# Two one-hot comparisons on VectorE: one wide operation of two tensors, or one operation a tile against a column of scalars

## The chip, the cores and the metric

The kernel runs on one core of one Trainium2 chip. The metric is the device time of one execution in microseconds; of the kernel before there are three, and their median is 2625.97 us. The profile is one more execution, recorded by the hardware.

## The reference, cut to what matters

A layer norm of x (12500 nodes, 256 features), a graph part and a feed-forward part with four experts, each with a residual:

```
time_feat = relu(edge_attr @ W_time.T + b_time)          # 212500 edges, 64 features
sums   = segment_sum(time_feat, src, num_segments=n)     # by the edge's source node
counts = segment_sum(ones, src, num_segments=n)
node_time_feat = sums / maximum(counts, 1)
fused = relu(concat(node_feat, node_time_feat) @ W_fusion.T + b_fusion)
x = x + (ln(x) + fused @ W_up.T + b_up)
x = x + shared_mlp(ln(x)) + top-2 of 4 experts(ln(x))
```

The change lies in the segment sum alone. `src` of this call is a list in no order that could be used as a segment order directly, so the kernel groups edges by bucket of 256 nodes.

## The kernel before

Edges are padded to 1664 tiles of 128. Two tiles make a group (256 edges), four groups a step, so there are 208 steps (`NS`) of eight tiles. Within a group VectorE sorts the edges by bucket (`sort_step`, lines 953 and 954 are its exchanges), which gives each edge a slot; three slots make one row of the table in DRAM.

All engines run one loop of 208 steps and meet through semaphores. In step s:

- VectorE prepares step s + 1 in `one_hots`: first `begun` (line 1119), for each of 4 groups a 128x128 matrix that says whether a bucket's blocks have begun at a row; then `slot_hot` (line 1127), for each of 8 tiles a 128x384 one-hot matrix of the edge's slot. Both compare a row of counted numbers in float16 (`iota_16`) with one number a partition and tile: the slot codes in `codes`, the beginnings in `begin`. The codes are written by ScalarE (line 1384) from PSUM, the beginnings by VectorE (line 860). Three buffers of each (`NSLOT`) let VectorE run ahead; `slot_hot` waits for TensorE's moves of three steps ago.
- TensorE computes features (line 597), takes high parts off (line 615), moves edges into their slots with `slot_hot` as the weights (line 611, six matmuls a group), and finds the rows of the table with `begun` (line 624).
- ScalarE applies the relu in three parts (line 1372), copies the moved rows out of PSUM (`keep_rows`, line 1378) into one of 12 buffers and the rows' numbers (`keep_dest`, line 1392) into one of 4.
- GpSimd issues four indirect DMAs a step (line 1564) that scatter the moved rows into the table. It also issues 36 that zero the ends of the tables (line 1553). Before a row buffer is written again, its scatter must have landed.
- From step 56 on, SyncE loads finished parts of the table, VectorE makes one-hots of the node within the bucket (line 1031), TensorE sums with them (line 640), and VectorE adds the sums (line 1051), in turns that `turn_at` spreads over the steps.

In the first steps VectorE also counts buckets (`count_bucket`, line 929), an operation of one tensor of 2-byte numbers and a constant, in runs of four without a wait between them. After the loop come the rest of the turns, and then from about 1757 us the node part in 25 groups, where line 1300 normalizes with two column scalars and line 1313 masks bits.

The order on every engine is that of the code; only waits move it in time. The two comparisons before are written as operations of two tensors, where the second repeats a pair of equal float16 numbers (`pairs`, `each_pair`, `in_pairs`): that is why `codes` and `begin` hold every number twice.

Of the kernel before, what the change touches and what calls it, by code (L numbers as in the profile page):

```python
# [6 lines left out]
P = 128  # L7
# [4 lines left out]
BLOCK = 3  # L12
# [13 lines left out]
def gnn_ffn(nc, x, src_e, src_g, attr, weights, dims, out):  # L26
    f32r, f16, u16 = mybir.dt.float32r, mybir.dt.float16, mybir.dt.uint16
    f32, bf16, i32 = mybir.dt.float32, mybir.dt.bfloat16, mybir.dt.int32
    ALU, ACT, AX = mybir.AluOpType, mybir.ActivationFunctionType, mybir.AxisListType
# [6 lines left out]
    GT, GS, GP = TILES_A_GROUP, GROUPS_A_STEP, GROUPS_A_SET  # L36
    G = GT * P
    NGR = ET // GT
    TS = GT * GS
# [13 lines left out]
    parts = [(set_cuts[k] * SPS, set_cuts[k + 1] * SPS) for k in range(NPARTS)]  # L53
    part_of = [k for k, (s0, s1) in enumerate(parts) for _ in range(s0, s1)]
    ng = [(s1 - s0) * GS for s0, s1 in parts]
# [30 lines left out]
    with ExitStack() as ctx:  # L86
# [7 lines left out]
        NATTR, NPAY, NROWS, NDEST, NTB, NSLOT, NXA, NIB = 3, 3, 12, 4, 4, 3, 3, 4  # L94
# [16 lines left out]
        s_slot, s_begun, s_dest_ps, s_dest, s_moved, s_rows = (sem(f"s_{n}") for n in ("slot", "begun", "dest_ps", "dest", "moved", "rows"))  # L111
# [75 lines left out]
        def carve(shape, dt, partitions=P):  # L187
            free = int(np.prod(shape))
            words = free if dt in (f32, i32) else (free + 1) // 2
            a = arena[0:partitions, top[0]:top[0] + words]  # L190
            top[0] += words
            assert top[0] <= ARENA, top[0]
            if dt != f32:
                a = a.bitcast(dt)[:, 0:free]
            if len(shape) == 1:
                return a
            names = "abcd"[:len(shape)]
            return a.rearrange(f"p ({' '.join(names)}) -> p {' '.join(names)}",
                               **dict(zip(names[1:], shape[1:])))

        hi = carve([ET], bf16)
        lo = carve([ET], bf16)
        codes = carve([NGR, GT, 2], f16)
        keys = carve([G, SETS], u16, GP)
        idx_key = carve([G], f32, GP)
        NGM, NCM = max(ng), max(n_ch)
# [2 lines left out]
        blocks_to = carve([NGM], f32)  # L209
        zeros_row = carve([NGM], f32)  # L210
        place = cnt_i.bitcast(f32)
        begin = [carve([n, 2], f16) for n in ng]
        hop = [carve([n, 2], bf16) for n in ng]
        col_i = carve([2], i32)
        col_f = carve([6], f32)
# [21 lines left out]
        iota_16 = carve([BLOCK * P], f16)  # L237
        slot_hot = [carve([TS, BLOCK * P], f16) for _ in range(NSLOT)]
        begun = [carve([GS, P], f16) for _ in range(NSLOT)]
# [80 lines left out]
        bank = [moved[:, 512 * i:512 * (i + 1)] for i in range(4)] + [ctx.enter_context(nc.psum_tensor(f"bank{i}", [P, 512], f32)) for i in range(4, 8)]  # L320

        def b3d(a, n, m):

            return a.unsqueeze(2).to_broadcast([a.shape[0], n, m])
# [5 lines left out]
        def pairs(a, n):  # L330
            return a.rearrange("p (c u) -> p c u", u=2).unsqueeze(1).to_broadcast([P, n, a.shape[1] // 2, 2])

        def each_pair(a, n):
            return a.unsqueeze(2).to_broadcast([P, a.shape[1], n // 2, 2])

        def in_pairs(a):
            return a.rearrange("p t (c u) -> p t c u", u=2)
# [88 lines left out]
        ZB, SB, MB = 4, (5, 6), 7  # L426
# [393 lines left out]
        def vector_program(e):  # L820
            def size_step(k, i):
                ps, n, m = bank[SB[0]], ng[k], n_ch[k]

                def sized(ins):
                    return ins.then_inc(s_size, 1)
# [31 lines left out]
                elif i == 9:  # L857
                    after("first")
                    sized(e.tensor_scalar(col_f[:, 3:4], col_f[:, 2:3], float(CH), None, ALU.mult))
                    sized(e.tensor_copy(begin[k], b3d(ps[:, 0:n], n, 2)))  # L860
                elif i == 10:
                    after("row0")
                    sized(e.scalar_tensor_tensor(place[:, 0:n], blocks_to[:, 0:n], col_f[:, 3:4], n_blocks[:, 0:n], ALU.add, ALU.subtract))
# [223 lines left out]
            for q in attr_in:  # L1087
                ins = e.memset(q[ONES_AT:ONES_AT + 1], 1.0)
# [23 lines left out]
            def one_hots(s):  # L1112
                k = part_of[s]
                if s == parts[k][0]:
                    e.wait_ge(s_size, size_no(k, "begin"))
                if s >= NSLOT:
                    e.wait_ge(s_dest_ps, s - NSLOT + 1)
                begin4 = begin[k][:, GS * (s - parts[k][0]):GS * (s - parts[k][0] + 1), :]
                e.tensor_tensor(in_pairs(begun[s % NSLOT]), pairs(iota_16[:, 0:P], GS), each_pair(begin4, P), ALU.is_ge).then_inc(s_begun, 1)
                if s % SPS == 0:  # L1120
                    e.wait_ge(s_codes, s // SPS + 1)
                if s == 0:
                    e.wait_ge(s_const, 2)
                if s >= NSLOT:
                    e.wait_ge(s_moved, GS * (s - NSLOT + 1))
                code8 = codes.rearrange("p g j u -> p (g j) u")[:, s * TS:(s + 1) * TS, :]
                e.tensor_tensor(in_pairs(slot_hot[s % NSLOT]), pairs(iota_16, TS), each_pair(code8, BLOCK * P), ALU.is_equal).then_inc(s_slot, 1)  # L1127

            one_hots(0)
            for step in range(n_steps):  # L1130
# [239 lines left out]
        def scalar_program(e):  # L1370
# [9 lines left out]
            def keep_codes(b, q):  # L1380
                q += sort_cuts[b]
                e.wait_ge(s_code_ps, q + 1)
                for j in range(GT):
                    ins = e.activation(codes[:, q * GP:(q + 1) * GP, j, :], b3d(bank[MB][:, j * GP:(j + 1) * GP], GP, 2), ACT.Copy)
                ins.then_inc(s_codes, 1)

            def keep_dest(s):
# [292 lines left out]
```

## Time and profile before

| | |
|---|---|
| median of 3 runs | 2625.97 us (2618.89 to 2632.24) |
| profiled execution, span of its instructions | 2387.8 us |
| outside of the span (median less span) | 238.2 us |
| TensorE matmul busy | 2163.3 us (91%) |
| VectorE busy | 1819.8 us (76%), 5481 instructions |
| ScalarE busy | 1324.4 us (55%) |
| GpSimd busy | 1222.2 us (51%), 944 instructions |

The profiled execution has no total of its own beside its span; what lies around the span is taken as the median less the span. In the tables of the trace, PE is TensorE, DVE VectorE, ACT ScalarE, POOL GpSimd and SP SyncE. A share of busy time is a mean over stages: GpSimd's 51% is made of some 1420 us in which it issues scatters and some 900 us in which it does almost nothing. Durations of VectorE instructions overlap a little: the next one's start is recorded before the end of the one ahead, so what an instruction costs its engine is the distance of two starts.

### The profile page before, as it was taken

How to read it: one execution, taken by the hardware profiler on the slowest of the kernel's cores; microseconds unless marked ns; L12 is line 12 of the kernel's file. 1: busy time of each engine (PE TensorE's matmuls, PEld its weight loads, DVE VectorE, ACT ScalarE, POOL GpSimd, SP SyncE). 2: the span in 40 equal slices, each digit the busy share in tenths (PEclk: the TensorE clock that was granted, in tenths of full speed). 3: DMA queues.
4: the chain of work that ended last, by engine and by line, in shares of the span. 5: the costliest groups of instructions: out<-in, count | busy, mean ns of one | idle time of the engine just before them, and what ended most of it. 6: DMA issues, size and time to landing. Idle time of an engine off the chain costs nothing.

```text
span 2387.8 us, 76843 instructions
## 1 busy us (share of the span) xinstructions
PE 2163.3 (91%) x28773; PEld 1798.7 (75%) x28773; DVE 1819.8 (76%) x5481; ACT 1324.4 (55%) x2833; POOL 1222.2 (51%) x944
## 2 busy tenths in 40 slices
PE   5778887789999999899999998888879999999998
PEld 1666665588988888799999998778756666676676
DVE  9987664687888987699998886899956656666565
ACT  1667776677878777777777776000023434344343
POOL 0787887888887888777788777000011111111110
PEclk7888988899999999999999999999989999999999
DMA  2263535456766666677777775777721111111111
GB/s 77 87 165 123 155 116 144 151 166 188 213 200 202 182 189 182 191 223 219 207 224 220 220 218 164 209 206 208 207 66 47 54 40 57 44 40 60 41 40 36
DMA packets 244429, 345.06 MB, mean 145 GB/s; under 512 B 34526, under 2 KB 218516, under 8 KB 243352
## 3 DMA queue, kind: packets, MB, share of 16 engines
q1 hardware_dynamic: 201252, 228.82, 35.0%
q0 software_dynamic: 42576, 110.49, 13.9%
q8 instruction: 232, 3.80, 0.7%
q14 instruction: 135, 1.11, 0.2%
q10 hardware_dynamic: 234, 0.85, 0.1%
HBM read 200.75 MB, written 186.38 MB: 162 GB/s over the span
## 4 chain that ended last, share of the span: by engine, by line
PE 60%; DMA 12%; issue 8%; DVE 8%; POOL 5%; ACT 4%; DVEq 2%; SPq 0%; POOLq 0%; ACTq 0%
PE bank L640 13%; PE moved L611 11%; PE bank L727 9%; DMA table<-arena 7%; PE moved L740 6%; PE bank L597 5%; POOL table L1564 4%; DMA arena<-table 4%; PE bank L615 3%; PE bank L735 2%; ACT arena L1378 2%; PE bank L813 2%; PE bank L769 2%; DVEq L1034 2%; ACT arena L1372 1%
## 5 line engine op out<-in xcount | busy, mean ns | idle before, releaser
L1564 POOL DMA_INDIRECT table<-arena x832 | 1093.8, 1315 | 338.7 <-issue 275.9
L1378 ACT ACTIVATE arena<-moved 128x588 bf16<-128x588 f32 x832 | 546.0, 662 | 193.3 <-PE moved L611 117.5
L611 PE MATMUL moved<-arena 128*128 128x196 bf16 x4992 | 602.5, 258 | 11.9 <-ACT arena L1378 10.8
L611 PEld LDWEIGHTS moved<-arena 128*128 128x128 f16 x4992 | 460.8, 99 | 94.8 <-ACT arena L1378 29.0
L1372 ACT ACTIVATE arena<-bank 128x512 f32<-128x512 f32 x624 | 372.2, 596 | 153.6 <-PE bank L597 124.9
L1127 DVE TENSOR_TENSOR arena<-arena 128x3072 f16<-128x3072 f16 x208 | 364.6, 1753 | 113.7 <-PE moved L611 112.4
L1051 DVE TENSOR_TENSOR sums<-sums,bank 128x130 f32 x912 | 259.0, 284 | 133.2 <-PE bank L640 120.3
L640 PE MATMUL bank<-arena 128*128 128x65 bf16 x8208 | 312.8, 194 | 34.7 <-DVE arena L1031 16.5
L640 PE MATMUL bank<-arena,w_all 128*128 128x65 bf16 x8208 | 309.9, 193 | 19.5 <-DVE sums L1051 10.1
L640 PEld LDWEIGHTS bank<-arena 128*128 128x128 bf16 x8208 | 290.7, 98 | 41.7 <-DVE arena L1031 30.3
L640 PEld LDWEIGHTS bank<-arena,w_all 128*128 128x128 bf16 x8208 | 288.3, 98 | 25.8 <-issue 12.9
L1031 DVE TENSOR_TENSOR arena<-arena 128x768 bf16<-128x768 bf16 x456 | 251.3, 552 | 33.6 <-DMA arena<-table 32.9
L1580 POOL TENSOR_TENSOR arena<-arena 128x4 f32<-128x4 f32 (+1 forms) x25 | 25.2, 1006 | 485.1 <-DVE arena L1287 485.1
L1031 DVE TENSOR_TENSOR w_all<-arena 128x768 bf16<-128x768 bf16 x456 | 250.9, 551 | 6.2 <-DMA arena<-table 5.9
L1468 ACT ACTIVATE arena<-bank,w_all 128x512 f32<-128x512 f32 (+1 forms) x225 | 152.9, 680 | 183.1 <-PE bank L727 145.1
L615 PE MATMUL bank<-arena,minus_ident 128*128 128x512 bf16 x416 | 172.4, 414 | 89.4 <-ACT arena L1372 88.7
L597 PE MATMUL bank<-w_all,arena 97*128 97x192 f32 (+1 forms) x1248 | 243.3, 333 | 3.5 <-ACT arena L1372 2.5
L1571 POOL TENSOR_TENSOR arena<-arena,w_all 128x1024 f32<-128x1024 f32 (+1 forms) x25 | 57.5, 2301 | 301.8 <-DMA arena<-x_ln 259.6
L597 PEld LDWEIGHTS bank<-w_all,arena 97*128 97x128 f32 x1248 | 208.1, 198 | 5.1 <-issue 3.4
L1482 ACT ACTIVATE arena<-bank 64x512 f32<-64x512 f32 (+1 forms) x25 | 14.2, 570 | 262.3 <-PE bank L754 262.3
L740 PE MATMUL moved<-w_all,arena 128*128 128x256 f32 x588 | 151.8, 403 | 1.2 <-DVE arena L1305 1.2
L727 PE MATMUL bank<-yt_high,w_high 128*128 128x512 f32 (+1 forms) x300 | 135.5, 452 | 0.0
(223 smaller groups left out, 2867.2 us busy)
## 6 DMA issues: line engine op xcount, KB each, us to landing
arena<-table SPq DMA_DIRECT2D x304, 441.0 KB
arena<-in_attr SPq DMA_DIRECT2D x208, 144.0 KB
table<-arena POOLq DMA_INDIRECT x832
x_ln<-arena SPq DMA_DIRECT2D x98, 128.0 KB
arena<-in_x SPq DMA_DIRECT2D x97, 128.0 KB
arena<-x_ln SPq DMA_DIRECT2D x24, 512.0 KB, 4.6
out_rows<-arena SPq DMA_DIRECT2D x24, 512.0 KB, 3.3
fused_node<-arena SPq DMA_DIRECT2D x98, 32.0 KB
```

Source lines behind the costliest of these rows:

```text
L597: mm = e.matmul(bank[ZB][:, q * 3 * A:q * 3 * A + w], attr_in[s % NATTR][0:ONES_AT + 1, q, :], wt[:, 0:w], start=q == 0, stop=True, skip_g ...
L611: mm = e.matmul(moved8[:, 4 * (n % 2) + h, 0:PW], slot_hot[s % NSLOT][:, t, h * P:(h + 1) * P], upper(s, 0, PW)[:, t, :], start=j == 0, st ...
L615: return e.matmul(z, minus_ident[:], upper(s, c0, A), start=False, stop=True, skip_group_check=True)
L640: mm = e.matmul(ps[:, v * SW:v * SW + w], one_hot, tab[t % NTB][:, c, r, c0 + at:c0 + at + w], start=i == 0 and at == 0, stop=i == CR * BL ...
L727: mm = e.matmul(bank[BH[(u - 1) % 2]][:, 0:w], weight(a, k), yt_halves[b][:, k, 0:w], start=i == 0, stop=i == len(terms) - 1)
L740: mm = e.matmul(half(BO, t), lhs[:, t * P:(t + 1) * P], rhs, start=first and t % 2 == 0, stop=done, skip_group_check=True)
L1031: e.tensor_tensor(in_pairs(hot[t % 2][:, c * PIECE:(c + 1) * PIECE]), pairs(iota_lo, PIECE), each_pair(lo_of, NODES_A_BUCKET), ALU.is_equa ...
L1051: e.tensor_tensor(d, d, sum_bank(t, c), ALU.add).then_inc(s_added, 1)
L1127: e.tensor_tensor(in_pairs(slot_hot[s % NSLOT]), pairs(iota_16, TS), each_pair(code8, BLOCK * P), ALU.is_equal).then_inc(s_slot, 1)
L1372: return e.activation(part_of_pay(s, c0, A), z, ACT.Relu)
L1378: e.activation(row_buf[n % NROWS], moved8[:, 4 * (n % 2):4 * (n % 2) + 3, 0:PW], ACT.Copy).then_inc(s_rows, 1)
L1564: e.indirect_dma_start(out=tables[k], out_offset=bass.IndirectOffsetOnAxis(ap=dest[s % NDEST][:, a:a + 1], axis=0), in_=row_buf[n % NROWS] ...
```

## The change

The two comparisons become operations of one tensor (`iota_16`) and one fp32 scalar a partition, read from a column of memory: 4 of 128 columns in place of one of 512 for `begun`, 8 of 384 in place of one of 3072 for `slot_hot`. Each run of them signals once, after its last. `codes` and `begin` hold each number once, in fp32, in as much memory as before; so ScalarE's copy of the codes and VectorE's copy of the beginnings write half the numbers.

```diff
-        codes = carve([NGR, GT, 2], f16)
+        codes = carve([NGR, GT], f32)
...
-        begin = [carve([n, 2], f16) for n in ng]
+        begin = [carve([n], f32) for n in ng]
...
-                    sized(e.tensor_copy(begin[k], b3d(ps[:, 0:n], n, 2)))
+                    sized(e.tensor_copy(begin[k], ps[:, 0:n]))
...
-                begin4 = begin[k][:, GS * (s - parts[k][0]):GS * (s - parts[k][0] + 1), :]
-                e.tensor_tensor(in_pairs(begun[s % NSLOT]), pairs(iota_16[:, 0:P], GS), each_pair(begin4, P), ALU.is_ge).then_inc(s_begun, 1)
+                for a in range(GS):
+                    g = GS * (s - parts[k][0]) + a
+                    ins = e.tensor_scalar(begun[s % NSLOT][:, a, :], iota_16[:, 0:P], begin[k][:, g:g + 1], None, ALU.is_ge)
+                ins.then_inc(s_begun, 1)
...
-                code8 = codes.rearrange("p g j u -> p (g j) u")[:, s * TS:(s + 1) * TS, :]
-                e.tensor_tensor(in_pairs(slot_hot[s % NSLOT]), pairs(iota_16, TS), each_pair(code8, BLOCK * P), ALU.is_equal).then_inc(s_slot, 1)
+                code8 = codes.rearrange("p g j -> p (g j)")[:, s * TS:(s + 1) * TS]
+                for t in range(TS):
+                    ins = e.tensor_scalar(slot_hot[s % NSLOT][:, t, :], iota_16, code8[:, t:t + 1], None, ALU.is_equal)
+                ins.then_inc(s_slot, 1)
...
-                    ins = e.activation(codes[:, q * GP:(q + 1) * GP, j, :], b3d(bank[MB][:, j * GP:(j + 1) * GP], GP, 2), ACT.Copy)
+                    ins = e.activation(codes[:, q * GP:(q + 1) * GP, j], bank[MB][:, j * GP:(j + 1) * GP], ACT.Copy)
```

On VectorE, at the loop's beginning (the first three steps' one-hots; the two lines between belong to the keys of the later sorts):

```order
-L1119 TENSOR_TENSOR arena<-arena 128x512
-L1127 TENSOR_TENSOR arena<-arena 128x3072
-L1119 TENSOR_TENSOR arena<-arena 128x512
-L1127 TENSOR_TENSOR arena<-arena 128x3072
-L1139 TENSOR_SCALAR arena<-arena 104x1792
-L1141 TENSOR_TENSOR arena<-arena 104x7x256
+L1120 TENSOR_SCALAR arena<-arena 128x128 x4
+L1130 TENSOR_SCALAR arena<-arena 128x384 x8
+L1120 TENSOR_SCALAR arena<-arena 128x128 x4
+L1130 TENSOR_SCALAR arena<-arena 128x384 x8
+L1143 TENSOR_SCALAR arena<-arena 104x1792
+L1145 TENSOR_TENSOR arena<-arena 104x7x256
```

Nothing changes its place; each pair of instructions becomes a run of 12 (an "x4" or "x8" is as many instructions in a row). On VectorE in a step with turns, first before and then now (line 1051 adds the sums of one chunk, line 1031 makes a one-hot, line 1049 keeps a register):

```order
L1051 TENSOR_TENSOR sums<-sums,bank 128x130
L1031 TENSOR_TENSOR w_all<-arena 128x768
L1034 TENSOR_LOAD offs
L1119 TENSOR_TENSOR arena<-arena 128x512
L1127 TENSOR_TENSOR arena<-arena 128x3072
L1049 ISA
L1051 TENSOR_TENSOR sums<-sums,bank 128x130
```

```order
L1051 TENSOR_TENSOR sums<-sums,bank 128x130
L1031 TENSOR_TENSOR w_all<-arena 128x768
L1034 TENSOR_LOAD offs
L1120 TENSOR_SCALAR arena<-arena 128x128 x4
L1130 TENSOR_SCALAR arena<-arena 128x384 x8
L1049 ISA
L1051 TENSOR_TENSOR sums<-sums,bank 128x130
```

Here too the run stands where the pair stood, and no other engine's order changes.

## Rows read from the trace of the kernel before

**Rows 1.** The page's 40 equal slices (59.7 us each): busy tenths of two engines.

```profile
PE   5778887789999999899999998888879999999998
...
POOL 0787887888887888777788777000011111111110
```

**Rows 2.** Stretches: from:to and length in us, busy us (instructions) by engine, then clock.

```profile
core 0: us, PE busy (x) PEld busy (x) DVE busy (x) ACT busy (x) POOL busy (x), PEclk, DMA share, GB/s
60.00:300.00 240.00, 190.18 (x1595) 150.55 (x1593) 192.52 (x492) 163.75 (x366) 192.27 (x142) 0.89 0.48 132
300.00:600.00 300.00, 246.33 (x2923) 208.39 (x2924) 199.84 (x487) 216.87 (x486) 243.92 (x185) 0.90 0.52 154
600.00:900.00 300.00, 284.95 (x4772) 261.70 (x4770) 264.82 (x666) 235.55 (x532) 244.53 (x183) 0.99 0.68 198
900.00:1200.00 300.00, 287.90 (x5001) 265.71 (x4998) 258.79 (x681) 231.40 (x520) 234.29 (x185) 0.99 0.70 205
1200.00:1475.00 275.00, 274.95 (x5117) 259.22 (x5115) 232.63 (x566) 206.03 (x458) 211.81 (x167) 1.00 0.75 216
```

**Rows 3.** The scatters on the page: count, busy us, mean ns, idle before them; then min/median/max.

```profile
L1564 POOL DMA_INDIRECT table<-arena x832 | 1093.8, 1315 | 338.7 <-issue 275.9
...
L1564 POOL DMA_INDIRECT table<-arena x832: 967/1034/7097, 64.8 to 1489.0; - x167
```

**Rows 4.** Waits (us, times, longest): POOL's in 300:900, then ACT's in 60:900.

```profile
POOL table L1564 <- issue: 87.2, 286, 0.3
...
ACT arena L1378 <- DMA table<-arena: 72.2, 54, 5.8
```

**Rows 5.** VectorE's groups by shape: busy us, mean ns, idle before and its releaser.

```profile
L1127 DVE TENSOR_TENSOR arena<-arena 128x3072 f16<-128x3072 f16 x208 | 364.6, 1753 | 113.7 <-PE moved L611 112.4 <-ACT arena L1384 1.3
...
L1119 DVE TENSOR_TENSOR arena<-arena 128x512 f16<-128x512 f16 x208 | 87.2, 419 | 0.7 <-issue 0.6
...
L1300 DVE TENSOR_SCALAR arena<-arena 128x256 f32<-128x256 f32 x98 | 33.8, 407 | 1.2 <-POOL arena L1580 1.2
...
L929 DVE TENSOR_SCALAR arena<-arena 128x624 bf16<-128x624 bf16 x98 | 24.9, 317 | 0.0
...
L929 DVE TENSOR_SCALAR arena<-arena 128x416 bf16<-128x416 bf16 x49 | 12.8, 261 | 0.0
...
L1313 DVE TENSOR_SCALAR arena<-arena 128x256 int32<-128x256 int32 x2 | 0.6, 286 | 0.0
```

**Rows 6.** VectorE in order of time near 83 us: start, duration, instruction, count.

```profile
82.34 1.01 DVE L929 TENSOR_SCALAR arena<-arena 128x624 bf16<-128x624 bf16 x4
83.27 0.42 DVE L1119 TENSOR_TENSOR arena<-arena 128x512 f16<-128x512 f16 x1
83.60 1.75 DVE L1127 TENSOR_TENSOR arena<-arena 128x3072 f16<-128x3072 f16 x1
```

**Rows 7.** VectorE and POOL in order of time near 1015 us.

```profile
1014.37 1.75 DVE L1127 TENSOR_TENSOR arena<-arena 128x3072 f16<-128x3072 f16 x1
...
1014.60 2.37 POOL L1564 DMA_INDIRECT table<-arena  x1 [0.30 <-issue]
```

**Rows 8.** The same beside a run of line 929, near 103 us.

```profile
102.77 1.01 DVE L929 TENSOR_SCALAR arena<-arena 128x624 bf16<-128x624 bf16 x4
...
102.42 1.49 POOL L1564 DMA_INDIRECT table<-arena  x1 [0.30 <-issue]
```

**Rows 9.** The same near 127 us.

```profile
126.06 1.01 DVE L929 TENSOR_SCALAR arena<-arena 128x624 bf16<-128x624 bf16 x4
126.98 0.42 DVE L1119 TENSOR_TENSOR arena<-arena 128x512 f16<-128x512 f16 x1
127.32 1.75 DVE L1127 TENSOR_TENSOR arena<-arena 128x3072 f16<-128x3072 f16 x1
...
126.17 3.74 POOL L1564 DMA_INDIRECT table<-arena  x1 [0.30 <-issue]
```

**Rows 10.** The same near 242 us.

```profile
241.26 0.98 DVE L929 TENSOR_SCALAR arena<-arena 128x624 bf16<-128x624 bf16 x4
...
241.62 1.01 POOL L1564 DMA_INDIRECT table<-arena  x1 [0.30 <-issue]
```

## The prediction

> **What bounds the kernel now.** I read the page's slices first. TensorE and GpSimd are both busy from about 60 to 1475 us; after that GpSimd is almost idle [rows 1]. The changed operations run only in these 1415 us, so what the change is worth is decided there. The table by stretches says more [rows 2]. GpSimd is busy 680.7 us of the 840 between 60 and 900 us, in 510 instructions. That looks like room, but each of its DMA instructions is preceded by 0.30 us in which it waits for nothing (the bracket in [rows 7]). Its waits of 300 to 900 us have 0.3 as the longest, so it never waits for data there [rows 4]. 510 x 0.30 = 153 us, and 680.7 + 153 = 834 of 840 us: GpSimd is full from 60 to 900 us. ScalarE meanwhile waits 72.2 us for scatters to land before it may reuse a row buffer [rows 4], and TensorE waits for ScalarE. From 900 to 1475 us GpSimd takes 446.1 + 352 x 0.30 = 551.7 of 575 us: 23 us are free, and TensorE, busy 563 of these 575 us, is the bound.
>
> In steps: four scatters a step. 60 to 900 us has 510 DMAs, about 37 of them for the tables' ends, so 473 / 4 = 118 steps; 900 to 1475 us has 352 / 4 = 88.
>
> Then VectorE. Its idle time is 540 - 392 = 148 us in 60 to 600 us and 875 - 756 = 119 us in 600 to 1475 us [rows 2], about 1.9 and 0.9 us a step. It runs ahead of TensorE: line 1127 waits 112.4 us in total for the moves that free its buffer [rows 5].
>
> **VectorE's own cost.** Line 929, one tensor of 2-byte numbers and a constant, takes 317 ns for 624 columns and 261 ns for 416 [rows 5]: 0.269 ns a column and 149 ns fixed. Four in a row start 0.93 us before what follows [rows 6], 0.233 each, so 84 ns of each duration lie under the next. The scalar from memory is priced by line 1300, 256 columns of fp32 with two such scalars, 407 ns, against line 1313, 256 columns of 4 bytes with none, 286 ns: 60 ns a scalar. So
> - 384 columns: 149 + 103 + 60 - 84 = 228 ns, x8 = 1.83 us, for 1.753 - 0.084 = 1.67 us before;
> - 128 columns: 149 + 34 + 60 - 84 = 159 ns, x4 = 0.64 us, for 0.33 us before [rows 6].
>
> Together 2.47 for 2.00 us, +0.47 us a step, 98 us in 208 steps. No row has a float16 tensor with an fp32 column. From below, a free scalar makes it 1.34 + 0.40 = 1.74 us (-0.26 a step). From above, half line 929's rate (2 columns where it has 4, as line 1313 has with 4-byte numbers) makes it 8 x 332 + 4 x 194 = 3.43 us (+1.43). I take 2.47: line 929 has the same sizes of elements, and line 1300 shows that a scalar adds a fixed term and leaves the rate of its 4-byte numbers alone.
>
> 0.47 is under VectorE's mean idle time of 0.9 or 1.9 us a step, and its buffers carry it over steps in which the sort fills it. What is exposed: about 1 us at the start, where TensorE waits for the first one-hots, and 2 or 3 us where sorting and turns meet. If that cover were gone (0.47 against 0.9), it costs up to 98 us.
>
> Line 860 (three times) and ScalarE's line 1384 (16 times) write half as many numbers: cast at nothing, bounds 0 and -2 us. The DMAs and waits stay where they are. The waits inside `one_hots` stand ahead of the first instruction of each run, so nothing new is queued behind them; the signal comes with the run's last instruction, which is in the sum above.
>
> **What the run does to GpSimd.** This is the term that decides. A scatter lasts 967 ns at least and 1315 on average [rows 3]. The excess, 348 ns x 832 = 290 us, has a visible cause. The scatter that starts 0.23 us after line 1127 lasts 2.37 us and ends at 1016.97, 0.85 us after line 1127 has ended [rows 7]. So a scatter touches something at its start that line 1127 holds, and does its 0.85 us of work when that is given back. Line 1127 comes 208 times and scatters follow each other every 1.27 us, so the first start falls on average 0.64 us into its 1.75 us: some 1.1 us of waiting a step. The excess of four scatters is 1.39 us a step in all, and other lines have a part in it; I take 1.0 us a step for the old pair.
>
> How does a run of one-tensor operations hold GpSimd? Line 929 is the only such run beside scatters.
> - It holds a scatter's end too: the one at 102.42 would have finished at 103.39, but ended at 103.91, 0.13 us after the run of four [rows 8]. Line 1127 doesn't do that.
> - It isn't given back between instructions of the run: at 103.27 a scatter should have reached its last part, an instruction of the run ended at about 103.55 and the wait went on. The scatter at 126.17 started inside a run and ended at 129.91, 0.84 us after line 1127 that followed it [rows 9].
> - It isn't strict: the scatter at 241.62 started inside a run and took 1.01 us [rows 10].
>
> The new run is 2.5 us long. With a touch at the start and one 0.85 us later, every 1.27 us, the first touch falls on average (0.85² + 0.42²) / (2 x 1.27) = 0.35 us into the run, and if nothing is given back it waits 2.5 + 0.1 - 0.35 = 2.2 us. I take 1.8, since some get through as in [rows 10]; that is an estimate. The bounds are 0.3 us (given back at each end, below) and 2.2 us. Against 1.0 us before, GpSimd takes +0.8 us more a step (-0.7 to +1.2).
>
> The sum: 118 steps in which GpSimd is full, x 0.8 = +94 us; 88 steps x 0.8 = 70, less the free 23, = +47 us; VectorE's start and dense places +3 us. +144 us on a span of 2387.8 is 2532; with the 238 us around the span, taken as unchanged, 2770 us. The longer steps also cover VectorE's 0.47.
>
> The Trainium skill (SBUF — State Buffer, SBUF: two separate sides) has VectorE and GpSimd share one pair of ports under an exclusive lock, taken by whichever starts first and held for the whole instruction. By it an instruction of 0.3 us is a wait of 0.3 at most. That the lock exists and that two tensors hold only GpSimd's reads agrees with [rows 7, 8]; that it ends with the instruction doesn't agree with [rows 9]. It is the first rival.
>
> **The rivals.**
> 1. The port is given back at the end of each instruction (faster). An operation of 0.31 us then holds a scatter 0.15 us on average, twice a step, 0.3 for 1.0 us before: GpSimd gains 0.7 us a step. Of 76 steps up to 600 us, 53 us come back, where TensorE is busy only 437 of 540 us. From 600 us TensorE is busy 94% and more, and 10 us are left to gain, which VectorE's 0.47 about eats. 2626 - 53 - 10 + 12 = 2575 us. For it: [rows 10], and the fixed 130 of 228 ns in which such an instruction hardly moves data. Against it: [rows 8, 9].
> 2. The scalar column halves the rate (slower still). The run is 3.4 us, it holds about 2.6 us, +1.6 a step: 208 x 1.6 - 23 = +310 us, 2935 us. Against it: line 1300 keeps the rate of its kind.
> 3. Nothing to be seen. The run is given back now and then, so that it holds about the 1.0 us of before, and VectorE's 0.47 lies in idle time: 2626 + 3 = 2629 us. For it: the mixed rows of line 929.
>
> The change does what it says, since the instructions can be seen in the order; that it would not isn't a case here.
>
> **The chances.** Forecast (held through most of the run) 0.58, its own range 2680 to 2870; rival 1 0.22; rival 2 0.07; rival 3 0.13. The predicted time is 2770 us. The range for 8 in 10 goes from 2570, about the middle of rival 1, to 2870: the forecast with the full 2.2 us, 208 x 1.2 - 23 = +227, gives 2853. No change is anything within 0.5% (13 us), about what a measurement of this kernel can tell. Slower: 0.58 + 0.07 + 0.03 of rival 3 = 0.68. Same: 0.10. Faster: 0.22.
>
> **What would show it.** Instructions of about 312 and 243 ns in lines 1130 and 1120, starts 228 and 159 ns apart; 560 ns or 400 ns mean rival 2's rate. The mean of a scatter at about 1315 + 200 = 1515 ns, and scatters that end 0.1 or 0.85 us after the run's last instruction; a mean near 1140 ns and no long ones is rival 1, one near 1315 rival 3. The slices should show GpSimd busy later than 1475 us, to some 1620, with TensorE's tenths lower in the same steps, and the node part after the loop as long as before (some 630 us). VectorE's waits for moves should be about as long as before or longer, since its cover grows. The forecast is wrong if the scatters' mean falls, or if the time moves while it stays.

## The result, and the profile after

The changed kernel takes 2701.8 us (median of 4 runs, 2695.45 to 2710.16), the kernel before 2626.5 on the same chip: 1.0305 times, 95% interval 1.0271 to 1.034. It is slower, as forecast, and by half of what was forecast (2770 us, 1.055 times).

The kernel before itself took 2382 to 2393 us in three comparisons, each on a chip of its own, and 2626 and 2665 us in two others, and the change does not do the same in both kinds; below they are called chips without and with stalls, though whether it is the chip is not shown.

The page after, first the slices (67.7 us each) that answer to [rows 1], then its chain and its groups. In the groups the columns are those of [rows 3] and [rows 5]:

```profile
PE   5678777788888888788888888878887999999999
...
POOL 0665555555554555454555554530000111111110
...
PE 61%; issue 9%; ACT 8%; DVE 7%; another core or an unknown queue 7%; DMA 4%; DVEq 1%; POOL 1%; SPq 0%; ACTq 0%; POOLq 0%
...
L1568 POOL DMA_INDIRECT table<-arena x832 | 908.7, 1092 | 850.0 <-ACT arena L1382 584.0
...
L1376 ACT ACTIVATE arena<-bank 128x512 f32<-128x512 f32 x624 | 373.3, 598 | 372.0 <-remote 223.1
```

GpSimd was to become fuller. It is emptier: its tenths fall from 7 or 8 to 5, a scatter takes 1092 ns on average for 1315 [rows 3], and its waits for ScalarE, none of which was over 0.3 us from 300 to 900 us, are 190.4 us there and 584 us in the whole run. Its last scatter ends at 1810 us, not at 1490. By its own sign the forecast is wrong here: the mean of the scatters falls. ScalarE in its turn waits for something that the trace calls remote, a source that it can't name; in the trace of before there was none of it. The same window as the POOL row of [rows 4] (waits from 300 to 900 us: sum, times, longest), and TensorE's from 60 to 2000 us:

```profile
POOL table L1568 <- ACT arena L1382: 190.4, 100, 5.6
POOL table L1568 <- issue: 72.0, 196, 1.4
...
PE bank L640 <- issue: 104.8, 234, 1.2
...
PE bank L597 <- issue: 13.4, 34, 1.1
```

TensorE is idle 104.8 us ahead of plain matmuls of line 640, 234 times, while it waits for nothing that the profile shows. Stretches that answer to [rows 2]:

```profile
300.00:600.00 300.00, 223.78 (x2096) 179.08 (x2097) 183.42 (x757) 189.29 (x418) 170.41 (x166) 0.84 0.42 126
600.00:900.00 300.00, 254.58 (x3818) 219.27 (x3817) 226.16 (x888) 190.69 (x429) 161.96 (x149) 0.97 0.52 160
900.00:1200.00 300.00, 250.38 (x3557) 213.27 (x3555) 224.19 (x844) 187.80 (x426) 157.84 (x146) 0.95 0.48 148
```

All four engines do less per 300 us than before [rows 2], so none of them is the bound that took over. VectorE's own rows, by shape and in order of time, answer to [rows 5, 6, 7]:

```profile
L1130 DVE TENSOR_SCALAR arena<-arena 128x384 f16<-128x384 f16 x1664 | 424.7, 327 | 155.8 <-PE moved L611 115.6 <-remote 33.2 <-issue 5.8
L1120 DVE TENSOR_SCALAR arena<-arena 128x128 f16<-128x128 f16 x832 | 171.1, 280 | 0.3 <-issue 0.2
```

```profile
1000.21 0.95 DVE L1120 TENSOR_SCALAR arena<-arena 128x128 f16<-128x128 f16 x4
1000.86 2.15 DVE L1130 TENSOR_SCALAR arena<-arena 128x384 f16<-128x384 f16 x8
1001.44 0.97 POOL L1568 DMA_INDIRECT table<-arena  x1 [0.30 <-issue]
...
1002.93 0.41 DVE L953 TENSOR_TENSOR arena<-arena 104x256 f32<-104x256 f32 x1
```

Four begun comparisons take 1000.86 - 1000.21 = 0.65 us (0.64 forecast), eight slot comparisons 1002.93 - 1000.86 = 2.07 us (1.83 forecast; 0.26 each, not 0.228). The scatter at 1001.44 starts in the middle of that run and takes its least time, 0.97 us. The forecast had it held to the end. That scatter is also why the run is long: in this trace 16 runs of eight have no scatter beside them, and they last 1.93 us at the median, so 1.85 us without the 0.08 us under the next instruction, as forecast.

### The profile page after: what moved, and what is told of

It is laid out like the page before. It is cut to its first block, busy times and chain, and to the rows that moved or that the text cites. A ratio compares the mean times of both kernels' runs of the same rounds, so it can differ in the third digit from the quotient of the medians.

```text
span 2708.4 us, 78923 instructions
## 1 busy us (share of the span) xinstructions
PE 2306.0 (85%) x28773; PEld 1863.2 (69%) x28773; DVE 1950.4 (72%) x7561; ACT 1325.9 (49%) x2833; POOL 1030.9 (38%) x944
## 4 chain that ended last, share of the span: by engine, by line
PE 61%; issue 9%; ACT 8%; DVE 7%; another core or an unknown queue 7%; DMA 4%; DVEq 1%; POOL 1%; SPq 0%; ACTq 0%; POOLq 0%
PE moved L611 13%; PE bank L640 12%; PE bank L727 8%; PE moved L740 6%; PE bank L597 6%; PE bank L615 3%; DMA arena<-table 3%; ACT arena L1382 3%; PE bank L624 2%; ACT arena L1376 2%; PE bank L735 2%; PE bank L813 2%; PE bank L769 2%; DVEq L1034 1%
## 5 line engine op out<-in xcount | busy, mean ns | idle before, releaser
L1568 POOL DMA_INDIRECT table<-arena x832 | 908.7, 1092 | 850.0 <-ACT arena L1382 584.0
L611 PE MATMUL moved<-arena 128*128 128x196 bf16 x4992 | 629.6, 264 | 40.5 <-ACT arena L1382 28.9
L1130 DVE TENSOR_SCALAR arena<-arena 128x384 f16<-128x384 f16 x1664 | 424.7, 327 | 155.8 <-PE moved L611 115.6
L640 PE MATMUL bank<-arena 128*128 128x65 bf16 x8208 | 339.4, 195 | 79.0 <-issue 55.0
L640 PE MATMUL bank<-arena,w_all 128*128 128x65 bf16 x8208 | 333.6, 194 | 66.8 <-issue 52.9
L640 PEld LDWEIGHTS bank<-arena 128*128 128x128 bf16 x8208 | 304.3, 99 | 98.3 <-issue 74.9
L597 PE MATMUL bank<-w_all,arena 97*128 97x192 f32 (+1 forms) x1248 | 274.4, 357 | 21.5 <-issue 13.4
L597 PEld LDWEIGHTS bank<-w_all,arena 97*128 97x128 f32 x1248 | 229.3, 215 | 35.1 <-issue 32.9
L1120 DVE TENSOR_SCALAR arena<-arena 128x128 f16<-128x128 f16 x832 | 171.1, 280 | 0.3 <-issue 0.2
L615 PEld LDWEIGHTS bank<-arena,minus_ident 128*128 128x128 bf16 x416 | 41.3, 99 | 148.9 <-ACT arena L1376 108.7
```

Source lines behind the costliest of these rows:

```text
L597: mm = e.matmul(bank[ZB][:, q * 3 * A:q * 3 * A + w], attr_in[s % NATTR][0:ONES_AT + 1, q, :], wt[:, 0:w], start=q == 0, stop=True, skip_g ...
L611: mm = e.matmul(moved8[:, 4 * (n % 2) + h, 0:PW], slot_hot[s % NSLOT][:, t, h * P:(h + 1) * P], upper(s, 0, PW)[:, t, :], start=j == 0, st ...
L615: return e.matmul(z, minus_ident[:], upper(s, c0, A), start=False, stop=True, skip_group_check=True)
L640: mm = e.matmul(ps[:, v * SW:v * SW + w], one_hot, tab[t % NTB][:, c, r, c0 + at:c0 + at + w], start=i == 0 and at == 0, stop=i == CR * BL ...
L1130: ins = e.tensor_scalar(slot_hot[s % NSLOT][:, t, :], iota_16, code8[:, t:t + 1], None, ALU.is_equal)
L1568: e.indirect_dma_start(out=tables[k], out_offset=bass.IndirectOffsetOnAxis(ap=dest[s % NDEST][:, a:a + 1], axis=0), in_=row_buf[n % NROWS] ...
```

## The experiments

Each ratio is to the kernel before on the same chip, with its 95% interval; "traced span" is that of the one profiled execution.

**The kernel before, again.** No edit.

> The kernel before, unchanged, for a second profile of it on a chip it shares with the next three. Open after the first comparison: the profiled execution of before had a span of 2387.8 us beside a median of 2626.5 us, the one of after a span of 2708.4 us beside a time of 2710.2 us. Theory A (the 238 us lie outside the span): the new span is near 2390 us again and its time near 2626. Theory B (the first profile of before was of an unusually quick execution): the new span is near 2620 us, and it shows the stalls that after has, in which TensorE waits for nothing that the profile shows (0.4 to 1.2 us before line 640) and ScalarE waits for an unknown releaser. I expect B, at 0.8. Ratio 1.00.

Measured: 2388.18 us, traced span 2389.1; the 19 runs of before on this chip have a median of 2391.57. Neither expectation fits. There is nothing outside the span here, and in the changed kernel's traced run the time is 2710.16 for a span of 2708.4. So the 238 us that the prediction put around the span do not exist: the trace shown was of an execution near 2390 us, the times shown were of others.

**The slot comparison alone.** `begin` and line 1119 stay as before:

```
-                e.tensor_tensor(in_pairs(slot_hot[s % NSLOT]), pairs(iota_16, TS), each_pair(code8, BLOCK * P), ALU.is_equal).then_inc(s_slot, 1)
+                for t in range(TS):
+                    ins = e.tensor_scalar(slot_hot[s % NSLOT][:, t, :], iota_16, code8[:, t:t + 1], None, ALU.is_equal)
+                ins.then_inc(s_slot, 1)
```

> Only the slot comparison as 8 operations of one tensor and a column; the beginnings stay one operation of two tensors. VectorE pays 8 x 0.23 for 1.67 us. Theory port (GpSimd held through runs): most of the 3.05%, since the longest run stays: +2 to 2.5%. Theory instruction count (more instructions on VectorE delay the fetching of all engines' instructions): 7 of 11 added instructions a step, +1.9%. Theory VectorE time (its own 0.47 us a step decide): 0.17 of 0.47 us, +1.1%.

Measured: 2314.78 us, 0.9675 (0.9657 to 0.9693). All three theories had it slower, and all three are wrong on this chip. Scatters 1105 ns on average; before on this chip 1332.

**The begun comparison alone.** The edit of the diff at lines 1118 to 1121, with `codes` as before.

> Only the comparison of beginnings as 4 operations of one tensor and a column; slots stay as before. Theory port: a run of 0.65 us ahead of the old 1.75, up to +1%. Theory instruction count: 3 of 10 or 11 added instructions a step, +0.8 to 0.9%. Theory VectorE time: 0.3 of 0.47 us, +2%.

Measured: 2383.88 us, 0.997 (0.9954 to 0.9985), scatters 1312 ns. Only the port theory's "up to +1%" comes near: by itself this part is almost nothing.

**Two tensors, by the tile.** The same twelve instructions a step as the change, but each still of two tensors:

```
+                for t in range(TS):
+                    ins = e.tensor_tensor(in_pairs(slot_hot[s % NSLOT][:, t:t + 1]), pairs(iota_16, 1), each_pair(code8[:, t:t + 1], BLOCK * P), ALU.is_equal)
```

> The kernel before with its two operations of two tensors cut by group and tile: 4 + 8 instructions of two tensors, as many instructions as after, about 2.65 us of VectorE a step (8 x 0.265 + 4 x 0.13) for 2.47 in after, and no one-tensor run. Theory port by one-tensor runs: near 1.00 or below, since short pieces free GpSimd more often. Theory instruction count, or VectorE time: 1.03 to 1.035, as after. This run tells the one-tensor form apart from the number of instructions and their time.

Measured: 2456.45 us, 1.0287 (1.0246 to 1.0327). Its page and its waits (sum, times, longest):

```profile
L1568 POOL DMA_INDIRECT table<-arena x832 | 1181.7, 1420 | 316.2 <-issue 266.1
```

```profile
ACT arena L1382 <- DMA table<-arena: 104.4, 76, 6.8
ACT arena L1396 <- DMA table<-arena: 95.4, 66, 4.6
```

GpSimd held longer is what the forecast had in mind, and this is how it looks: scatters at 1420 ns, ScalarE waiting some 200 us for them to land (126 us in the kernel before on this chip), 2.9% lost. By the expectation the ratio would speak for the number of instructions or for VectorE's time. Neither holds: the changed kernel, below, has as many instructions and as much VectorE time (1945 us busy, here 1959) and gains 1.8% on a chip without stalls. So the reading that GpSimd bounds this loop was right. Nor does cutting the operation give the port back between the pieces. This scatter starts with the run of eight and ends at 488.33, 0.85 us after the last of the eight:

```profile
485.25 2.23 DVE L1130 TENSOR_TENSOR arena<-arena 128x384 f16<-128x384 f16 x8
485.27 3.06 POOL L1568 DMA_INDIRECT table<-arena  x1 [0.30 <-issue]
```

**The changed kernel, on another chip.**

> The changed kernel, unchanged, timed again. The kernel before took 2626 us in the first comparison and 2391 us in the second, with the same program. If the 3.05% loss belongs to the change: ratio 1.03, some 2465 us, with TensorE stalls ahead of line 640 and ScalarE waits for an unknown releaser in its trace. If it belongs to the conditions in which both were timed at first: no such stalls, scatters near 1.1 us, VectorE 0.3 us a step more than the run with slots only (0.9675), so 0.975 to 0.985 when the kernel before takes 2390 us; and 1.02 to 1.03 if it takes 2626 us here. I expect the second.

Measured: 2337.42 us for 2382.34 before, 0.9816 (0.9795 to 0.9838): faster. Scatters 1124 ns. The chain of its page, and TensorE's waits from 60 to 2000 us:

```profile
PE 60%; DVE 21%; DMA 5%; DVEq 5%; issue 5%; ACT 2%; POOL 1%; SPq 0%; ACTq 0%; POOLq 0%
```

```profile
PE bank L640 <- DVE sums L1051: 32.9, 46, 5.0
...
PE bank L640 <- issue: 10.4, 19, 1.3
```

TensorE's waits for nothing are gone (10.4 us for 104.8), there is no wait on a remote source, and VectorE has 21% of the chain, against 8% in the kernel before (2389.1 us span).

**A constant for the column.** The codes are not read, so the output isn't the reference's:

```
-                    ins = e.tensor_scalar(slot_hot[s % NSLOT][:, t, :], iota_16, code8[:, t:t + 1], None, ALU.is_equal)
+                    ins = e.tensor_scalar(slot_hot[s % NSLOT][:, t, :], iota_16, float(t), None, ALU.is_equal)
```

> As after, but the slot comparison is with a constant of the instruction and not with the column: the moved rows are not those of the reference. It leaves out the reading of the column. VectorE: 8 x 60 ns less a step. Theory gap (GpSimd gets the port because an instruction that reads its scalar from memory leaves it free for a while, unlike line 929 in the profile of before): scatters rise from about 1.1 to 1.5 us or more on average and the time rises to 1.03 or more of before. Theory release (the port is given back between instructions anyway): scatters stay at 1.1 us and the time falls with VectorE's 0.48 us a step, to 0.96.

Measured: 2321.38 us, 0.9737 (0.9716 to 0.9758); the instruction takes 269 ns for 330. Neither of the expectation's two theories fits as it stands. The scatters take 1198 ns for 1124, so the run without the column holds GpSimd more, and here too some are held through it. This one starts 0.15 us ahead of the eight and ends at 128.38, 0.12 us after the last of them:

```profile
126.68 1.70 POOL L1568 DMA_INDIRECT table<-arena  x1 [0.30 <-issue]
126.83 1.43 DVE L1130 TENSOR_SCALAR arena<-arena 128x384 f16<-128x384 f16 x8
```

That is what [rows 8] showed beside line 929, which has a constant too. But the run is 0.5 us shorter, and the kernel is faster all the same. The same kernel on a further chip, as a partner of one below:

> The slot comparison as eight one-tensor instructions against a constant, run before on another chip (0.9737 there), as the partner of the one above. Theories 'number' and 'work' both: 1.02 to 1.035 of the kernel before where that takes 2600 us or more, 0.97 to 0.978 where it takes 2380 to 2400 us. If it is 0.97 to 1.00 where the kernel before takes 2600 us or more, the loss there hangs on the column operand, which neither theory says.

Measured: 2320.7 us for 2392.59, 0.9704 (0.9675 to 0.9732). Scatters 1190 ns. This chip had no stalls, so it says nothing on the two theories.

**Before, after and the slot part on one chip with stalls.** Three kernels as above, with no new edit.

> The kernel before, unchanged, for its profile beside the two below on one chip. Theory A (conditions: in the first comparison every engine's supply of instructions stalled, and the kernel before with it): if this chip takes 2600 to 2650 us for it, its profile has TensorE idle at L640 after nothing (issue) for 80 to 130 us instead of the 9.5 us of the profile shown, and ScalarE and VectorE waits ended by 'remote'. Theory B (the stalls come with the one-tensor instructions alone): a time of 2600 us or more with a span near 2390 and under 15 us of such idle time. If the chip takes 2380 to 2400 us, neither is told apart, and the run is only the base for the two below.

> The changed kernel, unchanged. Theory A: on a chip where the kernel before takes 2600 to 2650 us, this takes 1.025 to 1.035 of it; where it takes 2380 to 2400 us, 0.978 to 0.985 of it (2335 to 2360 us), with scatters of 1090 to 1130 ns mean on either. Theory B: 1.02 to 1.04 on any chip, the last pair having been a chance.

> Only the slot comparison is one-tensor, the begun comparison reads two tensors as before. Theory 'the begun part costs VectorE time' (four instructions at 159 ns for one at 419 or 224 x 4 us begun, on a VectorE without idle time): this is faster than the changed kernel on the same chip by 0.3 us x 88 steps = 25 us where the kernel before takes 2390 us (2305 to 2320 us). Theory 'the number of instructions meets the stalls' (7561 VectorE instructions in the changed kernel, 832 x 3/4 fewer... that is some 6900 here): on a chip where the kernel before takes 2600 to 2650 us this lies between, at 0.99 to 1.02 of it. Rival, that the two parts are independent of each other: 0.9675 + 0.003 for the changed kernel, so this and the changed kernel within 0.5% of each other.

Measured: before 2665.21 us (its profiled run 2662.21, span 2660.4); after 2738.42, 1.0269 (1.0219 to 1.032); slot part alone 2738.79, 1.0272 (1.0232 to 1.0311). The first comparison is repeated, and here the slot part alone loses as much as the whole change. TensorE's waits of 60 to 2000 us, of before and then of after:

```profile
PE bank L615 <- ACT arena L1372: 115.6, 103, 4.4
PE bank L640 <- issue: 71.8, 164, 1.2
```

```profile
PE bank L640 <- issue: 103.2, 231, 1.2
PE bank L615 <- ACT arena L1376: 96.8, 89, 5.6
```

The kernel before has the stalls too, fewer of them: theory A. One of them, in before:

```profile
1034.46 0.30 PE L640 MATMUL bank<-arena,w_all 128*128 128x64 bf16 x4 [0.44 <-issue]
...
1035.18 0.55 PE L640 MATMUL bank<-arena,w_all 128*128 128x65 bf16 x12 [0.42 <-issue]
...
1035.31 0.60 ACT L1372 ACTIVATE arena<-bank 128x512 f32<-128x512 f32 x1 [3.36 <-remote]
```

A few matmuls, 0.4 us of nothing, a few more, and ScalarE held 3.36 us beside it. I counted gaps of over 0.3 us ahead of TensorE's matmuls that nothing ended, from 60 to 1900 us, those less than 1.5 us apart as one stall, and took the loop's length from the first scatter's start to the last's:

| | loop us | stalls | scatter ns |
|---|---|---|---|
| before, 2388 us | 1433 | 11 | 1332 |
| after, 2337 us | 1372 | 15 | 1124 |
| slot part, 2315 us | 1351 | 11 | 1105 |
| before, 2662 us | 1702 | 123 | 1256 |
| after, 2738 us | 1770 | 161 | 1112 |
| slot part, 2739 us | 1779 | 178 | 1064 |
| after, 2702 us (first comparison) | 1744 | 165 | 1092 |

A few such gaps, 11 to 15, stand in the traces called without stalls too. The whole loss lies in the loop: what follows the last scatter takes 890 to 900 us in all seven traces. The loop's difference over the number of stalls comes out about the same for each kernel: (1702 - 1433) / 123 = 2.2 us, (1770 - 1372) / 161 = 2.5, (1779 - 1351) / 178 = 2.4. This is a division, and more than the gaps is in it. Of the 269 us between the two traces of before, TensorE is idle in 160; the other 109 are longer busy time (1400 us for 1291) for the same matmuls. From 60 to 1900 us the granted clock is at its lower level of 1.2 GHz for 270 us in 49 stretches, for 154 us in 26 on the chip without stalls. The change saves 61 us of the loop where there are no stalls. Where there are, it has 38 more of them (55 with the slot part alone), worth some 95 us, and each costs a little more (0.28 x 123 = 34 us): 95 + 34 - 61 = 68 us. That this is the loop's difference (1770 - 1702) comes of the way it was worked out and shows nothing more.

**One long one-tensor instruction**, against a constant (the codes are not read, so the output isn't the reference's):

```
+                e.tensor_scalar(slot_hot[s % NSLOT], iota_16.unsqueeze(1).to_broadcast([P, TS, BLOCK * P]), 3.0, None, ALU.is_equal).then_inc(s_slot, 1)
```

> The slot comparison is one one-tensor instruction of 3072 columns a step against a constant, in place of eight of 384 against a column: seven VectorE instructions a step fewer than the changed kernel, the codes not read (its output isn't the reference's). Theory 'number' (where the kernel before takes 2600 us or more, the 2080 VectorE instructions that the change adds lengthen the stalls): there this takes 0.97 to 1.00 of the kernel before. Theory 'work' (there the loss comes with one-tensor comparisons whatever their number): 1.02 to 1.035. Where the kernel before takes 2380 to 2400 us no theory sees stalls: 0.965 to 0.98 if the scatters get in beside a long one-tensor instruction too (mean 1090 to 1200 ns), 1.00 to 1.03 if that one holds them (mean 1350 to 1500 ns).

Measured: 2309.81 us for 2392.59, 0.9646 (0.9618 to 0.9674). The chip had no stalls, so 'number' and 'work' stay untold. The scatters:

```profile
L1566 POOL DMA_INDIRECT table<-arena x832 | 974.5, 1171 | 382.2 <-issue 195.0
```

```profile
214.28 0.96 DVE L1129 TENSOR_SCALAR arena<-arena 128x3072 f16<-128x3072 f16 x1 [1.95 <-PE moved L611]
214.66 1.43 POOL L1566 DMA_INDIRECT table<-arena  x1 [0.30 <-issue]
```

By the expectation's number (1090 to 1200 ns) scatters get in beside it; the rows say otherwise. The scatter of 214.66 ends at 216.09, 0.85 us after the instruction does, as the one in [rows 7] ended 0.85 us after line 1127. A long one-tensor instruction holds like the old one; it is short (1.01 us for 1.75), and that is why the mean falls.

**The old comparison, in eight pieces**: one instruction over 8 x 368 columns, seven over the last 16 columns.

```
+                W = BLOCK * P - 16
+                e.tensor_tensor(in_pairs(slot_hot[s % NSLOT][:, :, 0:W]), pairs(iota_16[:, 0:W], TS), each_pair(code8, W), ALU.is_equal)
+                for t, m in ((0, 2), (2, 1), (3, 1), (4, 1), (5, 1), (6, 1), (7, 1)):
+                    ins = e.tensor_tensor(in_pairs(slot_hot[s % NSLOT][:, t:t + m, W:]), pairs(iota_16[:, W:], m), each_pair(code8[:, t:t + m, :], 16), ALU.is_equal)
```

> The kernel before with its slot comparison still on two tensors, but cut into eight instructions: one over 8 x 368 columns and seven over the last 16 columns of a tile or two (7 more VectorE instructions a step, 5481 to 6937 in all, some 7 x 70 - 80 = 0.4 us more VectorE time a step, all of it still two-tensor). Theory 'number': 1.02 to 1.04 of the kernel before where that takes 2600 us or more. Theory 'work': 1.00 to 1.01 there. Where the kernel before takes 2380 to 2400 us: 1.00 to 1.015 by both, from the 0.4 us on a VectorE that has idle time left.

Measured: 2382.23 us for 2392.59, 0.9953 (0.9931 to 0.9975), a little better than the 1.00 to 1.015 expected. Scatters 1323 ns. No stalls on this chip either, so it doesn't decide between the theories; it shows only that seven more instructions a step cost nothing where there are none.

## Why the prediction was right in sign and wrong in its reasons

**What bounds the kernel: right for the trace it was read from.** GpSimd full to 900 us [rows 2 to 4] is borne out from both sides on chips without stalls: held longer, the kernel loses 2.9% (twelve two-tensor instructions); held less, it gains 1.8% at the same VectorE time (after), and 3.3% with the slot part alone. It does not hold where the 2626 us were measured. In the kernel before on the 2665 us chip GpSimd has, from 600 to 900 us, 187.4 us in 149 instructions:

```profile
600.00:900.00 300.00, 255.33 (x3822) 226.02 (x3823) 204.06 (x516) 192.25 (x430) 187.44 (x149) 0.94 0.53 159
```

187.4 + 149 x 0.30 = 232 of 300 us. GpSimd is not full there, so a faster scatter buys little.

**VectorE's own cost: the prices right, a wait put at nothing.** The begun part takes 0.65 us for 0.64. A slot instruction takes 310 ns at the median (312 forecast), and undisturbed its run lasts 1.92 us (median of the nine with no scatter beside them in the trace of 2331.5 us), so 1.84 us without the overlap for 1.83. What the sum left out is that a scatter which gets in holds VectorE up: over the loop the slot part takes 1.99 us a step on average. Together 2.64 against 2.00 us a step, +0.64, not +0.47. It isn't under other work once the scatters are fast: with it (both parts) the ratio is 0.9816, without the begun part's share 0.9675, on different chips. Apart, the parts give -3.25% and -0.3%; together -1.8%. So the begun part would cost about 1.4%, 34 us, on top of the slot part (by ratios of two chips; on the chip with stalls, where both kernels ran, they differ by nothing, 1.0269 and 1.0272), and VectorE's share of the chain goes from 8% to 21%. The forecast's +3 us for this was too small.

**The step that failed: "held through most of the run", +0.8 us a step.** A scatter meets VectorE at two places: at its start, and in its last part, 0.85 us later. I took the scatters of each trace, on chips without stalls, by where they meet the run of the slot comparison. "Held to the end" means that the scatter ended 0.85 us after the run's last instruction (met at its start) or 0.13 us after it (met in its last part):

| the run | starting in it, at least 0.15 us from its end | of these held to the end | starting up to 0.25 us ahead of it | of these held to the end | all scatters, mean ns |
|---|---|---|---|---|---|
| one of 3072, two tensors, 1.75 us (before) | 168 | 159 | 16 | 0 | 1332 |
| eight of 384, two tensors, 2.23 us | 189 | 89 | 25 | 0 | 1420 |
| eight of 384, with the column, 1.92 us and more (after) | 247 | 14 | 52 | 15 | 1124 |
| eight of 384, with a constant, 1.43 us and more (2320.7 us) | 128 | 23 | 60 | 33 | 1190 |
| one of 3072, with a constant, 0.96 us and more | 116 | 103 | 37 | 29 | 1171 |

A single instruction holds to its end. Back-to-back short ones do not simply give the port back: with two tensors or with a constant a large part of the scatters wait through all that is left of the eight. So the reading of line 929, which has a constant, was not wrong for a constant. What failed is that it was carried over to the form with the column. There most get through: those that start in the run take 0.97 us at the median and 1.14 on average (with two tensors in eight, 2.26 and 2.10). The only edit between the third row and the fourth is the operand, which also makes each instruction 61 ns shorter; why the column lets GpSimd in stays open. The other run with a constant (2321.4 us) has 18 of 120 and 30 of 62. A scatter can start within a run only if none was being held already, so the shares are no chances. Per step the scatters went from 4 x 1.332 to 4 x 1.124 us, -0.83 us, where the forecast had +0.8 and rival 1 -0.7. The size was too large as well: even with a constant, where the hold is as the forecast read it, the mean falls.

The Trainium skill (SBUF — State Buffer, SBUF: two separate sides) has the lock held for a whole instruction, and the prediction weighed that rule as rival 1. The rows agree for one long instruction (159 of 168, 103 of 116); that the wait would be over with the instruction does not fit the scatter of 3.06 us, which waited through eight instructions of some 0.35 us.

**Rival 1 has the sizes of what the change does where there are no stalls.** It gave 2575 of 2626 us, 0.981; measured is 0.9816. It had GpSimd gaining 0.7 us a step (0.83 measured) and VectorE's loss small. Its reason, that the port is given back at the end of each instruction whatever its form, is not what the table shows. So close an agreement has luck in it.

**The 238 us around the span: wrong.** Where a run takes that much longer, the time is lost inside the loop, beside the stalls (269 us between the two traces of before that have 11 and 123 of them). The trace given was of an execution that had next to none (9.5 us of TensorE waiting for nothing ahead of line 640). A loss of 144 us, nearly all at GpSimd, was added to them; neither term is what happened. The measured +75 us is of the forecast's sign, and 2702 us lies within its range, by luck: on a chip without stalls the same change saves 45 us.

**What makes 2702 us of 2626.** More stalls: 161 or 165 for 123. The slot part alone brings them (178). What a stall is stays open. For the supply of instructions speaks that TensorE, VectorE and ScalarE stop for nothing or for something remote, that a few matmuls come between gaps, and that half of the stalls of the slot-part kernel are 80 to 120 matmuls apart, while its instruction queue q8 moves 232 packets for 28773 matmuls, one in 124. But the packets of q8 take as long in either kind of trace (1.13 us on average without stalls, 1.15 to 1.17 with them), and the stalls don't line up with them: the 26 gaps counted in the traces of after and slot part without stalls all begin within 2 us of the end of a packet, the stalls anywhere between two packets. What another program on the chip may do to it no run here tells. Against a plain effect of number speaks that the slot part, with 6937 VectorE instructions, has more stalls than the whole change with 7561. It may be that engines which run faster between stalls meet every late delivery, where slower ones miss some. The three kernels that were to tell this apart met a chip without stalls, so it wasn't tried.

**A better version.** The slot part alone is the fastest kernel that computes all, 2314.8 us and 0.9675 of before, on a chip without stalls; with stalls it loses 2.7%, and of the kernels run there the one before stays the best.

## What to carry to other kernels

Compare the traced execution's span with the times before working out a sum: a gap of 10% is no constant around the span, it says that the trace shows another state than the one that is timed. Where VectorE and GpSimd meet, short one-tensor instructions let GpSimd in, but for the most part only the form with a column did so here: with two tensors, or with a constant, a run of eight can keep GpSimd waiting to its end. Each short one costs VectorE 0.04 to 0.08 us more than its share of one long instruction of two tensors, so look at which of the two is full in each part. And a behaviour read from one form of an instruction has to be tried on the form that is used. A gain that has been measured on one chip only is worth a second chip when the kernel has gaps that nothing ended.

## What the runs showed that I had not expected

- The same kernel takes 2382 to 2393 us in three comparisons and 2626 or 2665 us in two others, at nearly the same DMA work: queue q1 has 34.5% of 2389.1 us (824 us) and 30.5% of 2660.4 us (811 us).
- A float16 tensor with an fp32 column scalar costs VectorE 0.23 us for 384 columns when no scatter gets in (0.25 on average) and 0.16 for 128; with a constant in place of the column the duration of the 384 is 249 ns for 310 at the median (269 for 330 on average).
- Two-tensor instructions of 16 columns take 158 ns by duration, of 2944 columns 1686: (1686 - 158) / 2928 = 0.52 ns a column; and seven of the small ones a step don't slow a kernel whose VectorE has idle time.
- One constant comparison of 3072 columns takes 962 ns at the median, one of 384 takes 249: (962 - 249) / 2688 = 0.27 ns a column, so of the 249 ns some 147 are not the columns. The forecast had 0.269 and 149 from line 929.
- A run of eight two-tensor instructions of 0.35 us each holds a scatter for as long as 3.06 us; cut into pieces, the operation holds GpSimd more, not less (1420 ns for 1332).
